# Rows of the past without GpSimd, and half of the T splits and a table split put later in each group of channels

## The reference

```python
x = x + einsum('bct,bcd->bdt', x, W0[ids0])                  # 0: a 64x64 matrix per row
x = x + mask(t < len1) * (conv(x, K1) + x * D1)              # 1: long causal convolution, one kernel per channel
x = x + (x @ W2.T + bias + scale[id] * (x @ A[id].T) @ B[id].T)   # 2: 1024x1024 over t, plus rank 16
u = x * mask(t < len3)
x = x + mask(t < len3) * (conv(u, K3) + u * D3)              # 3: like 1, masked before and after
K = 2 * real(sum_n C' * exp(dtA * arange(T)))                # the kernels of 1 and 3
```

## Time and profile before

| | us |
|---|---|
| median of 3 runs | 1769.35 |
| lowest and highest run | 1765.36, 1769.8 |
| profiled execution | 1764.2 |
| its span, first to last instruction | 1762.4 |
| PE busy | 1537.9 (87%) |
| DVE busy | 1315.5 (75%) |
| POOL busy | 863.1 (49%) |
| ACT busy | 687.1 (39%) |
| mean granted clock of TensorE | 0.947 |

### The profile page before, as it was taken

How to read it: one execution, slowest core, us unless ns; L and a number is a source line. 1 busy time by engine, 2 the same in 40 slices (tenths; PEclk the granted TensorE clock), 3 DMA queues, 4 the chain that set the end, 5 groups by cost and what they waited for, 6 DMA issues and landing times.

```text
span 1762.4 us, 36790 instructions
## 1 busy us (share of the span) xinstructions
PE 1537.9 (87%) x14919; PEld 1313.7 (75%) x14919; DVE 1315.5 (75%) x1465; ACT 687.1 (39%) x1022; POOL 863.1 (49%) x389
## 2 busy tenths in 40 slices
PE   6777758798989898989898989989898989898996
PEld 6777746687868686868686877878687868686876
DVE  7897876877776767786868687777777776868763
ACT  4444533334334343434434333343433434343432
POOL 2111030647473928383645555564747382828354
PEclk9888888999989999999999999999999999999998
DMA  7899967466565757576765666565657575756434
GB/s 218 277 374 344 372 209 214 131 112 176 102 176 96 187 103 171 118 180 118 179 118 150 124 137 151 123 160 112 174 105 178 98 184 100 181 112 172 113 120 108
DMA packets 463687, 289.72 MB, mean 164 GB/s; under 512 B 339961, under 2 KB 419329, under 8 KB 461505
## 3 DMA queue, kind: packets, MB, share of 16 engines
q1 hardware_dynamic: 414336, 176.67, 45.3%
q10 hardware_dynamic: 49216, 110.98, 19.3%
HBM read 161.30 MB, written 75.96 MB: 135 GB/s over the span
## 4 chain that ended last, share of the span: by engine, by line
PE 49%; DVE 16%; issue 12%; DMA 12%; POOL 5%; ACT 3%; ACTq 1%; DVEq 0%; SPq 0%; POOLq 0%
PE ps L848 15%; PE ps L757 7%; DMA w2t<-w_scratch 7%; PE ps L801 7%; PE ps L931 5%; DMA arena<-in_x_dram 5%; DVE arena L1720 5%; DVE arena L1677 3%; PE ps L705 3%; PE ps L944 3%; PE ps L857 2%; PE ps L767 2%; PE ps L818 2%; POOL arena L565 2%; POOL arena L563 2%
## 5 line engine op out<-in xcount | busy, mean ns | idle before, releaser
L848 PE MATMUL ps<-arena,w2t 128*128 128x256 f16 x4608 | 555.9, 282 | 127.3 <-DMA w2t<-w_scratch 127.3
L848 PEld LDWEIGHTS ps<-arena,w2t 128*128 128x128 f16 x4608 | 464.0, 101 | 205.9 <-DMA w2t<-w_scratch 135.6
L585 POOL TENSOR_TENSOR arena<-arena 128x1024 f32<-128x1024 f16 x64 | 153.5, 2398 | 548.3 <-DMA arena<-arena 282.4
L1677 DVE SCALAR_TENSOR_TENSOR arena<-gbuf,arena 128x1024 f16<-128x1024 f32 x64 | 165.4, 2621 | 32.6 <-ACT arena L1171 32.6
L705 PE MATMUL ps<-arena 128*128 128x128 f32 x1024 | 144.4, 303 | 48.6 <-DVE arena L1575 27.4
L1250 ACT ACTIVATE arena<-arena 128x512 f16<-128x512 f32 x128 | 80.6, 630 | 249.6 <-DVE arena L1757 248.6
L705 PEld LDWEIGHTS ps<-arena 128*128 128x128 f32 x1024 | 135.6, 215 | 54.6 <-DVE arena L1575 30.6
L1761 DVE TENSOR_TENSOR arena<-arena 128x512 f16<-128x512 f32 x128 | 132.7, 1037 | 26.6 <-ACT arena L1250 25.1
L588 POOL TENSOR_TENSOR arena<-arena,one_xs 128x1024 f32<-128x1024 f32 x64 | 148.0, 2313 | 5.0
L1720 DVE SCALAR_TENSOR_TENSOR arena<-gbuf,arena 128x1024 f16<-128x1024 f32 x64 | 139.1, 2215 | 15.1 <-ACT arena L1229 15.1
L801 PE MATMUL ps<-arena 128*128 128x512 f16 (+1 forms) x768 | 137.0, 329 | 8.6 <-DVE arena L1643 8.6
(11 more groups left out here) (236 smaller groups left out, 2773.5 us busy)
## 6 DMA issues: line engine op xcount, KB each, us to landing
w2t<-w_scratch ACTq DMA_DIRECT2D x96, 512.0 KB, 4.3
arena<-in_x_dram SPq DMA_DIRECT2D x64, 512.0 KB, 8.0
out_dram<-arena SPq DMA_DIRECT2D x64, 512.0 KB, 3.8
gbuf<-x_scratch SPq DMA_DIRECT2D x120, 256.0 KB, 4.8
arena<-krow_scratch SPq DMA_DIRECT2D x32, 512.0 KB, 7.0
gbuf<-w_scratch ACTq DMA_DIRECT2D x32, 512.0 KB, 5.4
x_scratch<-arena ACTq DMA_DIRECT2D x14, 1024.0 KB, 9.6
x_scratch<-arena ACTq DMA_DIRECT2D x14, 896.0 KB, 7.5
```

What stands on the lines that cost most here:

```text
L585: nc.gpsimd.tensor_tensor(past[:, h % 2].rearrange("p (k t) -> p k t", k=NBLK), x3t[:, h % 2, 0], x3t[:, h % 2, 1], ALU.add).then_inc(past ...
L848: mm = nc.tensor.matmul(ps[:, bank, n * HW:(n + 1) * HW], weight(p, n, part, k), xx[:, :, k, :], start=(fresh and n == 0 and k == 0 and q ...
L1677: stt(lo[:, h], x1f[:, h], XS / FS, hi[:, h], ALU.mult, ALU.subtract).then_inc(x1_lo, 1)
```

## The change

`past_of` leaves GpSimd. ACT scales the hi part into the slot (`past_half`), DVE adds the lo part, scaled, in one instruction (`past_sum`). The `turn_x3` of h = 2, 3 wait for `past_ready` instead of `past_summed`. On DVE `t_split_lo` of quarters 3 and 4 moves from the end of a group to behind the low-rank rows of the next group, and quarters 1 and 2 go between `past_sum` and `take_past`. Their x1 loads move behind: part 0 behind store 1, part 1 behind store 2, parts 2 and 3 behind `load_g` at the end. `bases`, `table` of layer 1 and the splits of x1 move behind the second reads of partial sums, the x1 splits between the splits of x3.

```diff
@@ SP
                 for h in range(2, HG):
-                    sp.wait_ge(past_summed, HG * g + h - 1)
+                    sp.wait_ge(past_ready, HG * g + h - 1)
...
-                    if more2 and h == 1:
-                        load_group(g + 2)
+                    if more2 and h in (1, 2):
+                        load_part(g + 2, h - 1)
...
                     load_g(1, g + 1)
+                if more2:
+                    for n in range(2, 4):
+                        load_part(g + 2, n)
@@ GpSimd
-            def past_of(g):
...
                 make_tables(1, g)
-                past_of(g)
@@ ACT
+            def past_half(g, h):
+                n = HG * g + h
+                if h == 0:
+                    act.wait_ge(u_lo, made(1, g) + 1)
+                    act.wait_ge(v_made, 2 * made(1, g) + 2)
+                act.wait_ge(x3_turned[h], 32 * (g + 1))
+                at_least(act, c3_past, n - 1)
+                nc.scalar.activation(past[:, h % 2].rearrange("p (k t) -> p k t", k=NBLK), x3t[:, h % 2, 0],
+                                     ACT.Copy, scale=1.0 / XS).then_inc(past_hi, 1)
...
                     read_part(g, p, SUM_AT[p], 0, 0, 0)
-                if more1 and not early:
-                    bases_hi(0, g + 1)
...
                     read_part(g, p, MIX_AT[p], 2, NQ, 2, 3 + p)
-                if more1:
-                    for h in X1_ORDER[0:2]:
-                        x1_split_hi(g + 1, h)
...
-                if more1:
-                    for h in X1_ORDER[2:4]:
-                        x1_split_hi(g + 1, h)
+                if more1:
+                    bases_hi(0, g + 1)
+                    table_hi(0, g + 1)
+                    x1_split_hi(g + 1, X1_ORDER[0])
                 split_hi3(g, 0, 0, 0, 0)
                 if more1:
-                    table_hi(0, g + 1)
+                    x1_split_hi(g + 1, X1_ORDER[1])
                 split_hi3(g, 1, 0, 2, 1)
...
                 load_w(7)
+                if more1:
+                    x1_split_hi(g + 1, X1_ORDER[2])
                 split_hi3(g, 2, 2, NQ, 2)
...
+                    x1_split_hi(g + 1, X1_ORDER[3])
                 split_hi3(g, 3, 2, NQ + 2, 3)
-                bases_hi(1, g)
...
                 split_hi3(g, 4, 2, 0, 4)
+                bases_hi(1, g)
...
                     state_hi(1, g, 1)
+                    past_half(g, 0)
                     state_hi(1, g, 2)
+                    past_half(g, 1)
...
                                          ACT.Copy, scale=1.0 / FS).then_inc(c3_out, 1)
+                    if more1 and h in (1, 2):
+                        t_split_hi(g + 1, h - 1)
+                    if h in (1, 2):
+                        past_half(g, h + 1)
@@ DVE
+            def past_sum(g, h):
+                dve.wait_ge(past_hi, HG * g + h + 1)
+                past_row = past[:, h % 2].rearrange("p (k t) -> p k t", k=NBLK)
+                stt(past_row, x3t[:, h % 2, 1], 1.0 / XS, past_row, ALU.mult, ALU.add).then_inc(past_ready, 1)
...
+                if not early:
+                    for n in range(2, 4):
+                        t_split_lo(g, n)
...
+                if more1:
+                    bases_lo(0, g + 1)
+                    table_lo(0, g + 1)
                 add_part(0, 0, 0)
...
+                    x1_split_lo(g + 1, X1_ORDER[0])
+                lo3(0, 0, 0, 0)
+                add_part(1, 1, 1)
...
                     state_lo(1, g, 1)
+                    past_sum(g, 0)
                     take_conv1(g + 1, 0)
                     state_lo(1, g, 2)
+                    past_sum(g, 1)
                     take_conv1(g + 1, 1)
...
+                take_past(g, 0)
+                take_past(g, 1)
+                past_sum(g, 2)
+                if more1:
+                    t_split_lo(g + 1, 0)
+                take_past(g, 2)
+                past_sum(g, 3)
+                if more1:
+                    t_split_lo(g + 1, 1)
+                take_past(g, 3)
```

More of the change, by code:

```diff
@@ L468, in turn_x3, with load_part @@
                     sp.dma_start_transpose(x3t[:, h % 2, part], xx[:, h].rearrange("p k b -> p (k b)")).then_inc(x3_turned[h], 16)
[L470 to L476, removed]
+            def load_part(g, n):
+                h0, k0 = T_AT[n]
+                sp.wait_ge(t_lo, 4 * (g - 1) + n + 1)
+                for h in (h0, h0 + 1):
+                    load_x1(g, h, k0 // NQ)
+            for n in range(4):
+                load_part(1, n)
             def body(g, more1, more2):
@@ L1333, in body @@
                         state_hi(1, g, k)
+                    past_half(g, 0)
+                    past_half(g, 1)
                 for h in range(HG):
-                    if more1 and h == HG - 1:
-                        t_split_hi(g + 1, 0)
                     act.wait_ge(c3_summed, HG * g + h + 1)
@@ L1724, in _, with take_past @@
                 t_split_lo(0, n)
+            def past_sum(g, h):
+                dve.wait_ge(past_hi, HG * g + h + 1)
+                past_row = past[:, h % 2].rearrange("p (k t) -> p k t", k=NBLK)
+                stt(past_row, x3t[:, h % 2, 1], 1.0 / XS, past_row, ALU.mult, ALU.add).then_inc(past_ready, 1)
+            def take_past(g, h):
+                dve.wait_ge(c3_out, HG * g + h + 1)
+                dve.wait_ge(past_ready, HG * g + h + 1)
+                nc.vector.memset(gate[:, HG + h:HG + h + 1], 0.0)
+                nc.vector.copy_predicated(outt[:, h], past3[:, :], past[:, h % 2]).then_inc(c3_past, 1)
             def body(g, more1, more2):
@@ L1739, in body @@
                     combine_b(NBLK - 1, 1)
-                if more1 and not early:
-                    bases_lo(0, g + 1)
-                if more1:
-                    for h in X1_ORDER[0:2]:
-                        x1_split_lo(g + 1, h)
+                for h in range(HG):
+                    at_least(dve, x3_turned[h], 32 * g)
                 dve.wait_ge(lowd_hi, g + 1)
                 tt(lowdl, low_row[:, 0:HW], lowdh, ALU.subtract).then_inc(lowd_lo, 1)
-                for h in range(HG):
-                    at_least(dve, x3_turned[h], 32 * g)
                 def x3_quarter(xx, h0, row):
@@ L1808, in body @@
                         state_lo(1, g, k)
-                for h in range(HG):
-                    dve.wait_ge(c3_out, HG * g + h + 1)
-                    dve.wait_ge(past_ready, HG * g + h + 1)
-                    nc.vector.memset(gate[:, HG + h:HG + h + 1], 0.0)
-                    nc.vector.copy_predicated(outt[:, h], past3[:, :], past[:, h % 2]).then_inc(c3_past, 1)
-                    if more1 and h < 2:
-                        for n in ((0,), (1, 2, 3))[h]:
-                            t_split_lo(g + 1, n)
+                    past_sum(g, 0)
+                    past_sum(g, 1)
+                take_past(g, 0)
+                take_past(g, 1)
+                past_sum(g, 2)
+                if more1:
+                    t_split_lo(g + 1, 0)
+                take_past(g, 2)
+                past_sum(g, 3)
+                if more1:
+                    t_split_lo(g + 1, 1)
+                take_past(g, 3)
             for part in range(NPART):
```

33 lines of the change are left out of this document (12 added, 21 removed).

## The result

| | before | after |
|---|---|---|
| median, us | 1768.88 (1765.36 to 1769.8) | 1699.93 (1695.51 to 1700.59) |
| ratio, 95% interval | | 0.9608 [0.9587, 0.9629] |
| profiled execution, its span | 1764.2, 1762.4 | 1699.66, 1697.8 |
| PE busy | 1537.9 (87%) | 1544.3 (91%) |
| DVE busy | 1315.5 (75%) | 1340.3 (79%) |

69 us or 3.9% faster; the forecast was 1721, 48 us. In the changed kernel the lines have moved: L828 is now L814, L848 is L834, L757 is L743, L767 is L753, L801 is L787, L1237 is L1223, L1677 is L1678, L1720 is L1721, L1761 is L1773, L1814 is L1738, L561 is L563, L1206 is L1192, L1659 is L1660, L1653 is L1654, L1757 is L1769, L931 is L917.

A forecast was written before the change was run, and what follows sets the result against it. PE, gapless in its convolutions, loses 10.6 us a period in layer 2, mostly waiting for weights. Period 89.1 against 92.6 gives 49 over 14; with the ends 48 gained, median 1721, likeliest 1700 to 1745, 8 in 10 1645 to 1766.

The forecast's parts named there:

- The mechanism: Layer 2: last take 6.0 us earlier, GpSimd tables start 1041.9, `load_w(3)` issued 1047.7; the 6.1 us stop before SUM1 goes.
- The stop before the second MIX1: Layer 2 on PE: `load_w(7)` issued at about 1069.3, lands 1073.0, leaving 1.2 us of stop against 1.8.
- The new wait at the states: PE at layer 1's states, behind layer 2: waits for the reads and first split state, 4.8 us in all.
- The slow clock: PE matmuls behind the wait at the states: price 0 to 2.2 us a period, taken as 1.0.
- Three of four x1 splits contended: DVE queue behind `table_lo`: four x1 splits, three beside GpSimd at 2.64, one at 1.15, 9.1 us (4.6 to 10.6).
- The slip of the convolutions: PE convolutions: `near1(2)` 0.5 us late, second `past_sum` adds 0.15, so PE slips 0.65 per group.
- Group 0: First group: its `load_w(7)` stop of 9.24 waits behind more DVE work; 3 us lost, bounds -9 and +6.
- The end: Last group and after: group 15 gains 2 us; last rows quicker, but `turn_x3` waits for `past_sum(0)`: even, within 3.
- A: DVE keeps up: last split at 1086.3, no wait at states or slow clock; period 83.5, 127 gained, 1642; chance 0.22.
- B: Little gain: slow clock costs full 2.2, DVE stretch takes its late bound; period 91.5, 15 gained, 1752; chance 0.12.
- C: Slower: x3 transposes land late, ACT stands at `past_half(0)` and PE with it; at 7 late, 1786; chance 0.12.
- D: First wait in layer 2 stays because x1 loads hold up `load_w(3)`; no change; 0.06 with other null cases.

The follow-up runs named there:

- e1: Kernel before with only the past rows moved to ACT and DVE, T splits placed anew between takes, tables, x1 splits and loads in old places: 1699.41 us, 0.962.
- e2: Changed kernel with the rows of the past given back to GpSimd, all else as changed: 1744.33 us, 0.9887 of the kernel before.
- e10: Changed kernel with `bases_hi(1)` and `bases_lo(1)` one place earlier, ahead of the fifth split of x3: 1659.47 us, 0.9411 of the kernel before.
- e5: Changed kernel with `near1(g + 1, 1)` put ahead of `states(0, g + 1, 1)` on PE: 1645.85 us, 0.9329 of the kernel before.
- e11: Changed kernel with both swaps, `near1` ahead of the states and layer 1's bases ahead of the fifth x3 split: 1631.10 us, 0.9251 of the kernel before.
- e3: Changed kernel with the lo splits of T quarters 3 and 4 back at the end of the group before: 1696.01 us, 0.9603 of the kernel before.
- e6: Changed kernel with `past` in the memory of T quarters 3 and 4, so tables do not wait for the last take: 1707.78 us, 0.9679 of the kernel before.
- e7: e6 with layer 1 `bases` and `table` splits right behind first reads (ACT) and T splits (DVE), except group 0: 1637.48 us, 0.9287 of the kernel before.

## Why the prediction was right, and which of its terms were off

The predicted clock of the group began at 1034.55; read 31.08 earlier, it can be laid on the group of the profile shown above.

- **The mechanism** held: the takes end earlier, GpSimd starts its tables at 1010.24 (predicted 1010.8), `load_w(3)` goes out at 1016.71 (1016.6), and there is no stop before SUM1 and no slow clock there. e1 shows that the rows of the past carry the whole gain without the new order, e2 that without them two thirds of it go. What the prediction did not see is that the other parts, worth 21.5 us by themselves, add nothing beside them. It costed the path as a whole and not the past rows with the old order, where `load_w(3)` behind `bases_hi` leaves 3.5 us of stop, and the states are in time.
- **The stop before the second MIX1** was the term mis-sized for the sum: 1.2 predicted, 0.17 measured (1040.92). `load_w(7)` went out at 1037.36 (predicted 1038.2), and it had landed when PE came. That is 1.0 x 14, or 14 us, most of what the forecast was off by.
- **The new wait at the states** came where it was said, put down to ACT's reads of partial sums. The last split ended at 1059.15 (1060.5): the prediction's sum starts its 20.5 us, which run from the start of `table_lo`, at 1061.2, though it has that start at 1060 itself, so 1.2 are in it twice (`table_lo` started at 1029.26, which is 1060.3). Predicted were 4.8 us in all; it is 3.6 on the mean (50.1 / 14), with no stop for the first split state.
- **The slow clock** behind it was taken as 1.0; the L743 and L753 above cost 1.3 more in this group, and against the periods without any it is 1.5 (e10) or 1.6 (e5) on the mean. The states to the end of the period were predicted at 40.85 (4.8 + 1.0 + 34.4 + 0.65) and measured at 40.75: the stop was put 1.2 too high, the clock 0.5 too low, and some 0.6 are small gaps that no term has. That these cancel is luck.
- **Three of four x1 splits contended**: 2.35, 2.35, 2.78 and 1.21 us; taken were 2.64 and 1.15. The 0.8 for ACT and DVE waiting for each other at `bases(1)` is 1.1 by e10.
- **The slip of the convolutions**: `near1(2)` starts at 1072.71, behind a gap of 0.29, where 0.5 and 0.15 were taken.
- **Group 0** was even (95.85 against 95.95 us from its start to that of group 1) where 3 us of loss were taken: its stop at `load_w(7)` became 6.40 where it was 9.24, so the shift behind more of DVE that was feared does not show. **The end**, from the start of group 15, was 79.4 us against 84.3, 4.9 gained for 2 taken. In the end's row ACT did stand for the transposes, as said, yet it cost nothing in sum:

```profile
1688.36 1.06 ACT L1247 ACTIVATE arena<-arena 128x1024 f32<-128x1024 f16 x1 [4.12 <-DMA arena<-arena]
```

Added up: 14 x 1.1 more a period, 3 in group 0 and 3 at the end make 21, which is the distance from 1721 to 1699.9. That it comes out to the microsecond is luck: stage 0 was 4 longer in this execution, and the profiled execution lies at the median, not 5 under it. The gain was 1.4 times the forecast one, and 1699.9 stands at the very edge of the forecast's own range, 1700 to 1745.

- **The rivals.** A, DVE keeping up, did not happen in the change; e11 gets rid of the stop another way, and its 1631 stands beside the 1629 worked out for no stop at all. B took 2.2 for the clock, further from the 1.5 measured than the forecast's 1.0, and a late end of the stretch that did not come; its 1752 does not follow from its 15 us either, which give 1754. C came only at the very end, in the row above; ACT's wait for DMA before `past_half` is 4.1 us in the whole span, so in the periods the transposes were in time. D fell with `load_w(3)`, whose weights were there when PE came.

What stays open: periods of the changed kernel take from 87.04 to 88.68 us, those of e10 86.3 and 86.1 and then 85.3. The difference lies in how long the slow clock lasts: behind a stop of 3.6 us it cost 1.3 in one group and some 3 in another. What makes it short or long these rows don't show.

## What to carry to other kernels

Price what stands second behind a stop before the stop is removed: here some 11 us a period were won in one stage, 6.4 came back in the next, and a swap of two lines there gave 54 us more, where the change itself gave 69. When several parts are changed together, do each alone and each left out: one carried all the gain, and the others, worth 21.5 us without it, added nothing beside it until a further step was made. A stop costs its length and, where TensorE's clock comes down behind it, more: shortening one by 1.2 us gave 2.7 a period.

## What the runs showed of the hardware

- The stop of PE of 3.62 us was followed by 1.2 GHz, those of 2.41 and 1.47 by 2.4 GHz. The length alone does not decide it. Of e10's 14 stops of 2.27 to 2.53 us, two (2.47 and 2.40) had slow matmuls behind them, 24 in 2.23 and 2.74 us, and twelve had not, 1.51. In the kernel before, one of 2.85 was followed by full speed and one of 2.55 by 1.2 GHz. In the last group one of 2.52 was followed by slow matmuls in the changed kernel (24 of L917 in 3.73 us) and not in e10 (2.14). In e3 one of 3.46 (before L743 at 1055.40) had a granted clock of 0.85 in the 2 us behind it and 0.50 only in the 2 us after those.
- A DVE instruction of two SBUF inputs over 128x1024 took 1.21 alone and 2.35 to 2.78 beside GpSimd, two in a row 6.24; its neighbour that reads PSUM 0.68 in either place.
- Here the place of GpSimd's work beside DVE's counted for a lot: e6 and e7 build the same tables, the first of them beside the convolutions in both, and differ by 70 us. In e7 the second table is over before most of the splits of x1 and x3, in e6 it runs beside them.
